# Query and key tiles restacked through a DRAM scratch with large copies, and two thin matmuls cut into column tiles

## The reference

```python
h = layernorm(x) * (1 + ca) + sa
x = x + ga * attn_block(h)          # attention and an MLP, each with a residual
h = layernorm(x) * (1 + cb) + sb
x = x + gb * ffn(h)                 # gated FFN with 8 LoRA experts, top 2 chosen

# in attn_block: 32 heads of 8 features
qkv = rmsnorm(h) @ w_qkv.T
q, k = rope(q), rope(k)
attn = softmax(mask(q @ k.T / sqrt(8)))   # causal, inside blocks of 128 tokens
x = h + (attn @ v) @ w_o.T
x = x + (silu(gate) * value) @ w_down.T   # gate, value from rmsnorm(x) @ w_up.T

# in ffn: logits -> softmax -> top 2 of 8 experts
base = silu(x Wg) * (x Wu) Wd, and per chosen expert a LoRA correction of gate, up and down
```

## Time and profile before

| | us |
|---|---|
| median of 3 runs | 754.75 |
| lowest and highest run | 754.65, 755.93 |
| the profiled execution, its own time | 749.13 |
| its span, first to last instruction | 747.3 |

### The profile page before, as it was taken

One profiled execution on the slowest core, in us unless ns is written; L12 is line 12 of the kernel. 1 busy time (PEld: TensorE's weight loads), 2 busy tenths in 40 slices (PEclk: granted clock), 3 DMA queues, 4 the chain that ended last, 5 costly groups with the idle time before them and its releaser, 6 DMA issues.

```text
span 747.3 us, 12089 instructions
## 1 busy us (share of the span) xinstructions
PE 649.1 (87%) x4536; PEld 441.6 (59%) x4536; DVE 410.6 (55%) x617; ACT 321.7 (43%) x472; POOL 224.9 (30%) x292
## 2 busy tenths in 40 slices
PE   3770799899999899999999899999999899868996
PEld 2750355667785466657785466657785466637673
DVE  1553456367746564368646564368646564436544
ACT  3332245636544246526534246525533444414442
POOL 3023576204201476115001476115001674010000
PEclk9995799999999899999998799999999899977998
DMA  8245120002302100003202110003202100000000
GB/s 334 71 144 144 33 59 1 2 0 72 99 1 56 61 28 2 1 0 98 72 1 57 51 36 2 1 1 96 73 1 56 57 2 2 1 0 1 0 1 28
DMA packets 16466, 32.62 MB, mean 44 GB/s; under 512 B 5280, under 2 KB 5920, under 8 KB 16160
## 3 DMA queue, kind: packets, MB, share of 16 engines
q1 hardware_dynamic: 14880, 28.74, 12.8%
q0 software_dynamic: 1536, 3.15, 1.5%
HBM read 12.99 MB, written 2.10 MB: 20 GB/s over the span
## 4 chain that ended last, share of the span: by engine, by line
PE 64%; issue 13%; DVE 8%; ACT 7%; SPq 4%; POOL 2%; DMA 1%; DVEq 0%; POOLq 0%; ACTq 0%
PE bank L1424 7%; PE bank L1359 7%; PE bank L1259 7%; PE bank L1260 6%; PE bank L1261 6%; PE bank L1376 3%; PE bank L1402 3%; SPq L391 3%; PE bank L1565 3%; PE bank L1567 3%; PE bank L1566 2%; PE bank L1386 2%; PE bank L1456 2%; ACT tile_f L735 2%; ACT arena L636 2%
## 5 line engine op out<-in xcount | busy, mean ns | idle before, releaser
L1000 DVE TENSOR_REDUCE arena<-bank 128x8 f32<-128x1024 f32 x64 | 77.9, 1223 | 80.8 <-PE bank L1376 80.6
L1359 PE MATMUL bank<-mask 128*128 128x512 bf16 x256 | 83.5, 410 | 29.5 <-POOL k_wide L510 26.2
L1191 DVE TENSOR_TENSOR arena<-arena,bank 128x512 f32<-128x512 f32 (+1 forms) x72 | 49.1, 687 | 82.1 <-ACT arena L785 81.6
L1259 PE MATMUL bank<-n_hi,w_lo 128*128 128x512 f32 x200 | 86.4, 432 | 8.4 <-DVE n_lo L1055 6.0
L785 ACT ACTIVATE arena<-bank 128x512 f32<-128x512 f32 (+1 forms) x72 | 42.5, 596 | 102.1 <-PE bank L1567 53.5
L1260 PE MATMUL bank<-n_lo,w_hi 128*128 128x512 f32 x200 | 80.3, 401 | 0.0
L1261 PE MATMUL bank<-n_hi,w_hi 128*128 128x512 f32 x200 | 80.1, 401 | 0.0
L510 POOL TENSOR_TENSOR k_wide<-n_lo,head_of 128x512 fp32r<-128x512 f32 x32 | 33.1, 1039 | 153.1 <-PE bank L1567 139.4
L735 ACT ACTIVATE tile_f<-bank 128x1024 f32<-128x1024 f32 x64 | 64.2, 1023 | 33.5 <-PE bank L1402 33.4
L719 ACT CAST q_st<-bank 4x512 fp32r<-4x512 f32 x32 | 18.5, 579 | 115.4 <-PE bank L1386 115.4
L530 POOL TENSOR_SCALAR arena_r<-q_st,const 100x512 fp32r<-100x512 f32 x96 | 64.9, 693 | 0.2
(11 more groups left out here) (158 smaller groups left out, 1263.0 us busy)
## 6 DMA issues: line engine op xcount, KB each, us to landing
q_st<-arena_r SPq DMA_DIRECT2D x96, 64.0 KB, 2.0
k_st<-arena_r SPq DMA_DIRECT2D x48, 64.0 KB, 2.5
k_st<-arena_r POOLq DMA_DIRECT2D x48, 64.0 KB, 2.5
h_next<-in_x SPq DMA_DIRECT2D x4, 512.0 KB, 3.3
tile_f<-in_x SPq DMA_DIRECT2D x4, 512.0 KB, 4.3
out<-arena SPq DMA_DIRECT2D x4, 512.0 KB, 2.6
arena<-in_wmod SPq DMA_DIRECT2D x1, 1536.0 KB, 10.1
n_hi<-q_st SPq DMA_DIRECT2D x24, 64.0 KB, 2.0
```

What stands on the lines that cost most here:

```text
L1000: nc.vector.tensor_reduce(neg_max[:, 2 * a:2 * a + 2, MROW:KS], slot(("s1", n)).rearrange("p a (h s) -> p a h s", s=P), AX_X, ALU.max, neg ...
L1191: nc.vector.tensor_tensor(pair_tmp[n % 2][0:width], silu_out[n % 2][0:width], up, ALU.mult)\
L1259: nc.tensor.matmul(to, wl[rows, w_cols], ah[rows], start=start, stop=False)
L1359: nc.tensor.matmul(to, mask[:, 0, :], mask[:, which:which + 1, :].broadcast_to([P, GH, P]), start=True, stop=False)
```

## The change

`stack_tile` goes. All four tiles now travel through a DRAM buffer `scratch` (`rope_tiles` in the trace), which holds each tile's high and low part as 32 rows of 4 x 512 values. `keep` writes the two parts there, 256 KB each, with one DMA a part. `stack` reads a tile back with two DMAs: one for partitions 0 to 63 (512 KB; for q it reads the high part twice, through a dimension of size 2 and step 0) and one for 64 to 95 (256 KB). `highs_back` is one DMA of 256 KB from the scratch. SP issues them all; POOL issues none. A DMA that reads the scratch is issued after a wait for the writes (`kept`). The waits of ACT and DVE for the slots of the rope tiles become `half_kept`. The thin matmuls become four matmuls of 32 weight columns each, into four partition blocks of the output.

```diff
-        def stack_tile(engine, row, i, ahead):
-            half, is_k = i // 2, i % 2
-            engine.wait_ge(rope_hi.sem, rope_hi.count(row, i + 1, ahead))
-            engine.wait_ge(rope_lo.sem, rope_lo.count(row, i + 1, ahead))
...
-            for part, src in enumerate((hi, lo, hi) if is_k else (hi, hi, lo)):
-                for gq in range(GQ):
-                    engine.dma_start(dest[32 * part:32 * part + 32, half * GQ + gq, :].bitcast(F32),
-                                     src[32 * gq:32 * gq + 32, :].bitcast(F32)).then_inc(stacked[i].sem, 16)
+            def keep(i, row, ahead):
+                for part, ready in enumerate((rope_hi, rope_lo)):
+                    sp.wait_ge(ready.sem, ready.count(row, i + 1, ahead))
+                    sp.dma_start(scratch[i, part].rearrange("r (g s) -> g r s", g=GQ), rope_hl[i][part].bitcast(F32))\
+                        .then_inc(kept[i].sem, 16)
+            def stack(i, row, ahead):
+                half, is_k = i // 2, i % 2
+                slots = slice(half * GQ, (half + 1) * GQ)
+                sp.wait_ge(kept[i].sem, kept[i].count(row, 2 * 16, ahead))
+                dest = (k_st if is_k else q_st)[:, slots, :].rearrange("p g s -> p (g s)").bitcast(F32)
+                high, low = scratch[i, 0], scratch[i, 1]
+                two = bass.AP(high.tensor, high.offset, [[32 * GQ * S if is_k else 0, 2], [GQ * S, 32], [1, GQ * S]])
+                sp.dma_start(dest[0:64], two).then_inc(stacked[i].sem, 16)
+                sp.dma_start(dest[64:MROW], high if is_k else low).then_inc(stacked[i].sem, 16)
+            def stack_all(row, ahead):
+                keep(0, row, ahead)
+                for i in range(1, 4):
+                    keep(i, row, ahead)
+                    stack(i - 1, row, ahead)
+                stack(3, row, ahead)
             def highs_back(i, row, ahead):
...
+                sp.wait_ge(kept[i].sem, kept[i].count(row, 2 * 16, ahead))
+                sp.dma_start((k_high if is_k else q_high)[:, half, :].bitcast(F32),
+                             scratch[i, 0].rearrange("r (g s) -> g r s", g=GQ))\
+                    .then_inc(high_back[i].sem, 16)
...
@@ ACT, product_high @@
-                            half_stacked(act, row, j // 2, 1)
+                            half_kept(act, row, j // 2, 1)
@@ DVE, before lora_input(2) @@
-                        half_stacked(dve, row, 0, 1)
+                        half_kept(dve, row, 0, 1)
@@ PE, mean_squares (the router alike) @@
-                    last = nc.tensor.matmul(bank[:, norm.where, j:j + 1], tile_sum[:, j * P:(j + 1) * P],
-                                            con("mean")[:, 0:1], start=True, stop=True)
+                    for c in range(0, P, 32):
+                        last = nc.tensor.matmul(bank[c:c + 32, norm.where, j:j + 1],
+                                                tile_sum[:, j * P + c:j * P + c + 32],
+                                                con("mean")[:, 0:1], start=True, stop=True)
```

More of the change, by code:

```diff
@@ L198, in adaln_kernel @@
         eps_col = sb("eps_col", [P, 1])
-        pool_mark = sb("pool_mark", [P, 1])
+        scratch = nc.dram_tensor("rope_tiles", (4, 2, 32, GQ * S), F32).ap()
         bank = ctx.enter_context(nc.psum_tensor("bank", [P, 8, S], F32))
@@ L282, in adaln_kernel @@
         rope_lo = signal("rope_lo", 4)
[L283 removed]
+        kept = [signal(f"kept{i}", 2 * 16) for i in range(4)]
+        stacked = [signal(f"stacked{i}", 2 * 16) for i in range(4)]
         v_proj = signal("v_proj", 2)
         v_copied = signal("v_copied", 2)
[L286 removed]
+        high_back = [signal(f"high_back{i}", 16) for i in range(4)]
         heads_known = signal("heads_known", 0)
@@ L376, in half_stacked, with half_kept @@
             for i in (2 * half, 2 * half + 1):
-                engine.wait_ge(stacked[i].sem, stacked[i].count(row, PARTS * GQ * 16, ahead))
-        def stack_tile(engine, row, i, ahead):
-            half, is_k = i // 2, i % 2
-            engine.wait_ge(rope_hi.sem, rope_hi.count(row, i + 1, ahead))
-            engine.wait_ge(rope_lo.sem, rope_lo.count(row, i + 1, ahead))
[L384 to L388, removed]
-            for part, src in enumerate((hi, lo, hi) if is_k else (hi, hi, lo)):
-                for gq in range(GQ):
-                    engine.dma_start(dest[32 * part:32 * part + 32, half * GQ + gq, :].bitcast(F32),
-                                     src[32 * gq:32 * gq + 32, :].bitcast(F32)).then_inc(stacked[i].sem, 16)
+                engine.wait_ge(stacked[i].sem, stacked[i].count(row, 2 * 16, ahead))
+        def half_kept(engine, row, half, ahead):
+            for i in (2 * half, 2 * half + 1):
+                engine.wait_ge(kept[i].sem, kept[i].count(row, 2 * 16, ahead))
         block = ctx.enter_context(nc.Block())
@@ L451, in row_steps @@
                 sp.wait_ge(out_ready.sem, out_ready.count(row, 0))
-                half_stacked(sp, row, 1, 0)
-                sp.wait_ge(high_back[2].sem, high_back[2].count(row, GQ * 16))
+                half_kept(sp, row, 1, 0)
                 load(x_res, row, res_loaded)
                 if not last:
-                    stack(row, 1)
                     for half in range(2):
-                        half_stacked(sp, row, half, 1)
+                        half_stacked(sp, row, half, 0)
+                    for i in range(4):
+                        sp.wait_ge(high_back[i].sem, high_back[i].count(row, 16))
+                    stack_all(row, 1)
                     sp.wait_ge(gu_ready.sem, gu_ready.count(row, FF_STEPS.index((FT - 1, 0)) + 1))
@@ L466, in row_steps @@
                     .then_inc(stored.sem, 16)
-            stack(0, 0)
+            keep(0, 0, 0)
+            keep(1, 0, 0)
             sp.wait_ge(v_proj.sem, v_proj.count(0, 2))
-            for i in range(4):
-                sp.wait_ge(rope_hi.sem, rope_hi.count(0, i + 1))
+            for i in range(2):
                 highs_back(i, 0, 0)
+            for i in range(2):
+                stack(i, 0, 0)
+            for i in range(2, 4):
+                keep(i, 0, 0)
+            for i in range(2, 4):
+                highs_back(i, 0, 0)
+                stack(i, 0, 0)
             with sp.Fori(0, B - 1) as row:
@@ L503, in spread_keys @@
                     tile = high_back[2 * half + 1]
-                    pool.wait_ge(tile.sem, tile.count(row, GQ * 16, ahead))
+                    pool.wait_ge(tile.sem, tile.count(row, 16, ahead))
                 if u >= 2:
@@ L587, in row_steps @@
                         rope_cos(row, i, 1)
-                    stack_tile(nc.gpsimd, row, 3, 1)
                     first_units(row, 1)
@@ L1369, in scores_for_max @@
                         tile = high_back[2 * half]
-                        pe.wait_ge(tile.sem, tile.count(row, GQ * 16, ahead))
+                        pe.wait_ge(tile.sem, tile.count(row, 16, ahead))
                 to = fill(row, "s1", n)
```

19 lines of the change are left out of this document (5 added, 14 removed).

## The result

| | before | after |
|---|---|---|
| median of the runs, us | 754.7 (745.8 to 755.9) | 805.31 (800.1 to 806.3) |
| profiled execution, own time and span, us | 749.13, 747.3 | 806.28, 804.5 |
| mean granted clock | 0.943 | 0.906 |

The ratio is 1.0688, with a 95% interval of 1.0624 to 1.0753: the change makes the kernel some 51 us slower. Ratios here are formed from those runs of a kernel that lie within 1.5% of its fastest; the kernel before spreads over 742 to 756 us, so a ratio can differ from that of the medians.

A forecast was written before the change was run, and what follows sets the result against it. It took the prologue to be bound by the number of DMAs on SP, the passes not. Stalls 33 + clock 8 + first pass 8.5 + thin matmuls 1 = 50.5 us on 749.1, plus 5.6 to the median: 805, range 775 to 832.

The forecast's parts named there:

- the forecast (80%): Whole kernel: copies on few DMA engines delay what is queued behind them; 805 us, from 785 to 830 by itself.
- The number of engines: Scratch copies: a DMA is split along its outermost dimension, so `keep` and `highs_back` get 4 engines, the doubled q read 2.
- The stall of a pass: Three passes: ACT waits for `keep` 3, 10.9 us late each, 33 us in all, from 24 to 47.
- The clock: After each of four new idle stretches of PE: 2 us lost to a lowered clock, 8 us in all.
- The first pass: Prologue and first pass: `highs_back(3)` and `h_next` land late for POOL, so the pass ends some 8.5 us later.
- The thin matmuls: `mean_squares` and router cut in four: no change at full clock; +1 us in all, between -5 and +5.
- The sum: Whole kernel: 50.5 us on the profiled execution's 749.1 gives 799.6; with 5.6 to the median, 805.
- The copies get all 16 engines: Rival, 5%: all copies, whatever their outermost dimension; nothing is late, only the prologue's 13.3 us count: 741.5.
- `keep` 4, the read 16: Rival, 10%: `keep` uses 4 engines, the step-0 read 16; 2.5 us late a pass; 754, from 746 to 757.
- ACT's waits don't bind: Rival, 5%: in the passes, for instance because `keep` 3 passes the q read; only the first pass pays: 765.

The follow-up runs named there:

- q_read_split: The changed kernel with the doubled q read as two reads of 32 partitions, 256 KB each; 750.83 us, ratio 1.0046.
- keeps_first: The changed kernel with all eight writes of `keep` issued before the first read, in the passes only; 756.9 us, ratio 1.0109.
- all16: The changed kernel with the scratch laid out as the tiles lie in SBUF and each stack as three reads of 32 partitions; 727.35 us, ratio 0.9728.
- thin_only: The kernel before with only the thin matmuls (`mean_squares` and router) cut into four, stacking as before; 745.69 us, ratio 0.9958.
- q2_only: The kernel of all16 with q's high part doubled again by a step-0 outermost dimension, in four reads of 128 KB; 735.56 us, ratio 0.9766.

## Why the prediction came out right

Point by point, the forecast (80%) was the mechanism that happened, and 805 the time; but the terms were off in both directions.

- **The number of engines.** `keep` 4 (measured 4.1) and the step-0 read 2 (2.0), at 23 and 26 GB/s an engine: right, and q_read_split, keeps_first and all16 show each link. The rule of the Trainium skill ("DMA: Bandwidth & Descriptors", "Rules for kernel authors") on a zero-stride dimension says the same; no row of the trace before could show it, and the sign of the result hung on it.
- **The stall of a pass.** 10.9 us predicted, 14.3 measured. From the first write to the end of the 512 KB read it was 20.6 us by my queue, and about 22 in the trace (187.1 to 209); from there to the landing of `keep` 3 it was 16.1, and 17.9 in the trace (209 to 226.85). Together the last write landed some 3 us later than in the sum. Two things were not in my queue: SP was held, so `keep` 3 was issued only at 209.21, while from 205.50 to 208.00 just 2.0 engines were busy; and the copies on 16 engines have 8 KB packets of 0.65 us in the middle from 209 to 213, where those of the q read take 0.31. Which of them makes the 3 us, no run separates.
- **The clock.** 2 us for each new stretch, 8 in all; 2.7, 2.6 and 2.4 by the windows after the three stalls, 7.7.
- **The first pass.** 8.5 us predicted, 13.4 measured. Each milestone was in the right order and late: `k_wide` 63.76 for 62.75, `q_ex` 81.42 for 77.6, the key tile of the second half 112.09 for 105.2, L500 115.98 for 110.2, `q_ex` of unit 3 117.56 for 112.3.
- **The thin matmuls.** This step failed: +1 us predicted, with -5 as the lower bound, and about -6 measured (thin_only -3.2, all16 -5.9, the changed kernel -7.8 us by the ratios, whose intervals reach 3 to 6 us to either side; -8.7, -10.9 and -6.6 by the medians). I priced the narrow instructions by the row of L1424, 0.030 us each; they take 0.011, so a router takes 0.72 us and not 1.95. That row is of instructions with 128 columns of output, and these have 1 or 8. The Trainium skill, on the page "TensorEngine Tiling (Array Packing)", section "Key Properties", says that different tiles can load weights and multiply in parallel. The trace agrees: in thin_only a weight load of the router lasts 0.113 us (the median of L1504), yet one starts every 0.011 us, and the call falls from 1.81 to 0.72 us. The section "Instruction Overhead" of that page gives each matmul an overhead of some 60 cycles, so that one column takes as long as 60. If the narrow instructions ran one after the other at that, 25 ns at 2.4 GHz, a call of `mean_squares` would take an estimated 0.8 us; it takes 0.30.
- **The sum.** Stalls and clock 50.6 where I had 41, the first pass 13.4 where I had 8.5, thin matmuls -6 where I had +1; the three passes are 45.8 us longer, so some 5 us of the stalls were made up elsewhere; that this was at clock stretches, which wander anyway, is my reading and not shown. The sum against the profiled execution should have been 57 and was 50.5. The prediction still met the median, because I added the 5.6 us by which the profiled execution of before lay under its median, and the changed kernel's profiled execution does not lie under its own (806.28, 805.31). Two errors of 6 us cancelled there. That the forecast met the median to 0.3 us is luck; what it earned is the mechanism and the size of some 50 us.
- **The rivals.** "The copies get all 16 engines" gave 741.5: all16 is 727, and 738 with the thin matmuls as before. "`keep` 4, the read 16" gave 754: q_read_split is that kernel, 751. "ACT's waits don't bind" gave 765: keeps_first, 757. Each price was too high, the first by 14 us, of which the thin matmuls have 6 to 11, the others by 3 and 8.

Left open: how many descriptors a queue takes before it holds its engine, and why the thin matmuls gain more in some pairs of runs than in others.

## What to carry to other kernels

Fewer and larger DMAs pay only if the outermost dimension on both sides can be cut into 16: here 2 pieces ran on 2.0 engines and 4 on 4.1. Lay out the intermediate buffer for that, and don't put a step-0 copy of 2 outermost. The order of a queue is worth as much as its speed: in the passes a slow copy cost next to nothing until something urgent stood behind it on its engines, so issue what is waited for first (48 us here, without a faster copy). A matmul of 128 weight columns took 0.12 us for 1 column of output and 0.11 for 8, so the columns did not set its time; that its weight load does is my reading. Cutting the 128 weight columns into four tiles made the calls 2.5 to 3.4 times shorter.

## What was not expected of the hardware

- The engine that issues a DMA can be held in the issue while a slow read stands in the queue ahead or on the same DMA engines: 18.00 us for one issue on SP, 7.92 to 9.83 in the passes, 14.45 on ACT, against 0.5 normally. That the queues of these DMA engines were full is my reading. In q2_only, where the slow read came in four pieces, the longest single issues are 2.5 to 3.0 us.
- Two queues that meet on the same DMA engines are served packet by packet here. 8-byte packets of POOL's queue each waited for an 8 KB packet of SP's, 0.31 us, so that a copy with all its data through at 207 landed at 223.
- Copies of 8 KB rows to 32 or 64 partitions keep the 16 engines busy (93.6% from 209.00 to 213.00) with 0.65 us a packet in the middle, where the same packets take 0.31 on 2 engines.
- 32 matmuls of 32 weight columns for one column of output take 0.30 us at full clock and 0.65 at half; 8 of 128 weight columns 0.98 and 1.88.
